# Second biases of the experts as a product per tile, four sets of buffers for the late sums, two Relu's on ScalarE, and a new order of the instructions

## What is computed

```python
# first layer, the recurrence, per token t and feature
tau = max(u + k, eps); e1 = exp(eps - tau); e2 = exp(u + k - tau)
out = (e1 * alpha + e2 * v) / (e1 * beta + e2)
tau2 = max(eps - w, k); d1 = exp(eps - w - tau2); d2 = exp(k - tau2)
alpha, beta, eps = d1 * alpha + d2 * v, d1 * beta + d2, tau2
# second layer, the experts
logits = flat_x @ W_router + b_router
top_vals, top_idx = top_k(logits, 2)
router_weights = softmax(sparse_logits)
for e in range(8):
    h = relu(flat_x @ W1[e] + b1[e])
    y = h @ W2[e] + b2[e]
    final_output += y * (router_weights[:, e] * mask)[:, None]
x = x + gb * final_output
```

## Time and profile before

| | |
|---|---|
| median of 3 runs | 1699.84 us (1699.17 to 1706.25) |
| the profiled execution | 1700.76 us, of which 1698.9 us from the first to the last instruction |
| mean granted TensorE clock | 0.889 |
| busy: PE, DVE, ACT, POOL | 1363.7, 1147.9, 968.7, 548.3 us |
| transfers | 217.67 MB |

### The profile page before, as it was taken

The page is one execution under the profiler, slowest core; times in us unless marked ns, Lnnn a source line. Parts: engine busy times, 40 slices in busy tenths (PEclk is TensorE's granted clock), DMA queues, the critical chain, the costliest instruction groups (busy, mean ns, idle before and its releaser), DMA issues. The chain is left out here.

```text
span 1698.9 us, 26885 instructions
## 1 busy us (share of the span) xinstructions
PE 1363.7 (80%) x8390; PEld 875.3 (52%) x8390; DVE 1147.9 (68%) x3024; ACT 968.7 (57%) x2279; POOL 548.3 (32%) x589
## 2 busy tenths in 40 slices
PE   3466887878879788999999878988999987983862
PEld 1233453434445335776666434556666655773761
DVE  4568788887989867758878887868674744141103
ACT  1344665656666456777777555656756654752440
POOL 1123221312132473122212236444151143325335
PEclk7677998979999878999999888799998998997995
DMA  4012134142211334555554222354645676887762
GB/s 120 7 35 72 37 121 157 47 129 68 89 52 47 89 103 124 155 164 161 146 177 133 71 76 75 108 155 132 176 136 152 174 202 191 268 267 239 213 198 63
DMA packets 202005, 217.67 MB, mean 128 GB/s; under 512 B 17402, under 2 KB 167493, under 8 KB 199560
## 3 DMA queue, kind: packets, MB, share of 16 engines
q1 hardware_dynamic: 193672, 199.17, 39.9%
q0 software_dynamic: 8192, 16.79, 3.1%
HBM read 161.18 MB, written 53.94 MB: 127 GB/s over the span
## 5 line engine op out<-in xcount | busy, mean ns | idle before, releaser
L1525 DVE TENSOR_REDUCE cmx<-bank 128x2 f32<-128x512 f32 x512 | 329.4, 683 | 94.4 <-PE bank L1148 80.2
L854 ACT ACTIVATE wide<-bank 128x512 f32<-128x512 f32 x512 | 278.9, 607 | 113.6 <-PE bank L1164 106.4
L1164 PE MATMUL bank<-wide 75*128 75x512 bf16 x512 | 182.5, 421 | 31.8 <-ACT wide L854 19.4
L1148 PE MATMUL bank<-wide 72*128 72x256 bf16 x1024 | 179.8, 285 | 29.3 <-DVE cmx L1525 23.0
L715 POOL DMA_INDIRECT x_slots<-sx,sslot x128 | 128.0, 1000 | 111.7 <-DMA x_slots<-sx,sslot 49.5
L1180 PE MATMUL bank<-wide,bva 128*32 128x512 f32 x1024 | 150.3, 668 | 14.6 <-ACT wide L854 9.6
L1148 PEld LDWEIGHTS bank<-wide 72*128 72x128 bf16 x1024 | 91.5, 101 | 131.6 <-issue 56.7
L734 POOL DMA_INDIRECT kg<-y_slots,sslot x104 | 101.2, 973 | 160.5 <-issue 49.6
L893 ACT ACTIVATE mH<-bank,mW 128x128 f32<-128x128 f32 x376 | 107.6, 375 | 55.6 <-PE bank L989 50.3
L1164 PEld LDWEIGHTS bank<-wide 75*128 75x128 bf16 x512 | 50.1, 106 | 154.8 <-ACT wide L854 84.6
L989 PE MATMUL bank<-mT,mW 128*128 128x128 f32 x872 | 122.8, 285 | 7.0 <-DMA mW<-in_wexp 2.2
(11 more groups left out here) (293 smaller groups left out, 2798.3 us busy)
## 6 DMA issues: line engine op xcount, KB each, us to landing
mW<-in_wexp SPq DMA_DIRECT2D x109, 514.0 KB
wide<-q_parts SPq DMA_DIRECT2D x32, 576.0 KB
inner<-in_wexp SPq DMA_DIRECT2D x31, 514.0 KB
wide<-in_wexp SPq DMA_DIRECT2D x16, 514.0 KB, 4.1
mX<-x_slots SPq DMA_DIRECT2D x27, 256.0 KB, 4.2
y_slots<-mX SPq DMA_DIRECT2D x27, 256.0 KB, 4.3
q_parts<-bp SPq DMA_DIRECT2D x32, 192.0 KB, 2.2
x_slots<-mH SPq DMA_DIRECT2D x2, 3072.0 KB, 10.9
```

What stands on the lines that cost most here:

```text
L854: act.activation(cP[:, i % 8, :], bank[seat["G_s", i]][:, :], ACT.Exp, scale=SCALE).then_inc(S["c_p"], 1)
L1148: ins = pe.matmul(ps[:, j * T:(j + 1) * T], cQ[0:SROWS, z, h, tt * P:(tt + 1) * P], cK[0:SROWS, z, h // G, :], start=True, stop=True)
L1164: pe.matmul(ps[:, :], cK[0:KROWS, z, g, sc_ * P:(sc_ + 1) * P], cQ[0:KROWS, z, h0:h0 + 2, :], start=True, stop=True).then_inc(S["c_s2"], 1)
L1525: dve.tensor_reduce(cmx[:, u % 2, tt, 2 * hp:2 * hp + 2], bank[seat["C_s", i]][:, :].rearrange("p (j t) -> p j t", j=2), AX_X, ALU.max, ne ...
```

## The change

1. The second biases. K_w, K_b and the copy between them are gone, 16 of each, and with them the first addition of K_out and the three operations of R_info that made weights by expert (L1600, L1602, L1604). In their place each tile gets one product of 24 rows in bf16, ahead of its M_d: the stationary operand is a column of a new array `which` (1 where the tile's expert is the row's), spread over 128 columns, the moving one is b2 as three bf16 parts. A step I_erow makes the parts at the start, and one more instruction in S_tile makes `which`.
2. The sets of the K stage. Chunks 0 to 9 use set 0; chunks 10, 11, 12, 13, 14 and 15 use sets 1, 2, 3, 0, 1 and 2. A gather waits only for the store of the last chunk in its own set, and the first use of sets 1 to 3 for the end of stage R_c of the last chunk.
3. E_y ends after the two differences. ACT makes Relu(z) and Relu(-z) and then both Exp's.
4. ORDER is another table on all engines.

```diff
-    "M": ("R_h R_lg S_pre K_w K_b M_t M_u".split(), (7,)),
+    "M": ("R_h R_lg S_pre M_t M_u".split(), (7,)),
...
+TURNS = FIRST_CHUNK[-2] - 1
+        k_sets = [max(c - TURNS, 0) % 4 for c in range(CHUNKS)]
         def k_set(c):
-            return (0, c + 1) if c <= LATE else (c - LATE, 1)
+            return k_sets[c], k_sets[:c + 1].count(k_sets[c])
...
                     if s == "K_g":
-                            if z == 0 and c:
-                                pool.wait_ge(S["k_st"], 16 * c)
+                            if n > 1:
+                                pool.wait_ge(S[f"k_st{z}"], 16 * (n - 1))
+                            elif z:
+                                pool.wait_ge(S["r_h0"], CHUNKS)
...
                     if s == "E_exp":
+                        act.wait_ge(S["e_ky"], i + 1)
+                        act.activation(aP[:, :, :, :], aQ[:, 1:3, :, :], ACT.Relu).then_inc(S["e_m"], 1)
                         act.wait_ge(S["e_m"], 2 * i + 1)
+                        act.activation(aQ[:, 1:3, :, :], aQ[:, 1:3, :, :], ACT.Relu, scale=-1.0).then_inc(S["e_m"], 1)
                         act.activation(aP[:, :, :, :], aP[:, :, :, :], ACT.Exp, scale=-1.0).then_inc(S["e_exp"], 1)
                         act.wait_ge(S["e_m"], 2 * i + 2)
-                        act.activation(aQ[:, 1:3, :, :], aQ[:, 1:3, :, :], ACT.Exp).then_inc(S["e_exp"], 1)
+                        act.activation(aQ[:, 1:3, :, :], aQ[:, 1:3, :, :], ACT.Exp, scale=-1.0).then_inc(S["e_exp"], 1)
...
                 def mlp_out(i, z, ps):
                     pe.wait_ge(S["m_r"], FC * (i + 1))
+                    g = place(i)[0]
+                    if i == FIRST_TILE[g]:
+                        pe.wait_ge(S["s_tile"], 2 * (g + 1))
+                    j = i - FIRST_TILE[g]
+                    pe.matmul(ps[:, 0:P], which[:, g, j:j + 1].broadcast_to([BROWS, P]), eb2[:, :],
+                              start=True, stop=False)
                     for c in range(FC):
-                                        weights[w_slot(i)[0]][:, o:o + D], start=(c == 0), stop=(c == FC - 1))
+                                        weights[w_slot(i)[0]][:, o:o + D], start=False, stop=(c == FC - 1))
...
                         dve.scalar_tensor_tensor(aQ[:, 2, :, :], aE[:, :, 0:T], negw[:, 0:1],
                                                  k_ps, ALU.add, ALU.subtract).then_inc(S["e_ky"], 1)
-                        dve.wait_ge(S["e_ky"], i + 1)
-                        dve.tensor_scalar(aP[:, :, :, :], aQ[:, 1:3, :, :], 0.0, None,
-                                          ALU.max).then_inc(S["e_m"], 1)
-                        dve.tensor_scalar(aQ[:, 1:3, :, :], aQ[:, 1:3, :, :], 0.0, None,
-                                          ALU.min).then_inc(S["e_m"], 1)
...
                     if s == "K_out":
-                        dve.wait_ge(S["k_b"], i + 1)
...
-                        v(dve.tensor_tensor(g_[:, 0, :, :], g_[:, 0, :, :], tiles(bank[seat["K_b", i]]), ALU.add))
...
 ORDER = {
...
-        K_b K_w K_b
+        W_d W_u W_d W_u W_d W_u W_d W_u W_d W_u W_d*2
```

More of the change, by code:

```diff
@@ L425, in program @@
             mask3 = rz[0:PARTS, 0, 0:PARTS]
+            eraw, eb_1, eb_2 = (rz[0:BROWS, k, :] for k in range(1, 4))
+            epart = cP[0:BROWS, 6, :].bitcast(BF16).rearrange("p (k d) -> p k d", d=D)[:, 0:PARTS, :]
+            esum = [cP[0:BROWS, 7, k * D:(k + 1) * D] for k in range(2)]
+            part_of = rhn[0:BROWS, 0, 0:PARTS]
+            turns = rhn[0:BROWS, 1, 0:BROWS]
             MOD = (3, 4, 5, 6)
@@ L454, in program @@
                 *[(colk[b * KR:(b + 1) * KR, :], rows_of_keys(a["cols"])) for b in range(BC)],
[L455 removed]
+                (rev[:, :], a["c_rev"]), (upper[:, :], a["c_upper"]),
+                *[(rz[k * EXPERTS:(k + 1) * EXPERTS, 1, :], a["L1_ffn_b2"]) for k in range(PARTS)],
                 (restart[:, :], a["c_restart"]), (steps16[:, :], a["c_steps16"]), (steps1[:, :], a["c_steps1"]),
@@ L622, in _ @@
                         sp.wait_ge(S["k_out"], i + 1)
-                        sp.dma_start(rows(a["out"], i), kg[k][:, 0, :, :]).then_inc(S["k_st"], 16)
-                sp.wait_ge(S["k_st"], 16 * CHUNKS)
+                        sp.dma_start(rows(a["out"], i), kg[k][:, 0, :, :]).then_inc(S[f"k_st{k}"], 16)
+                for k in range(4):
+                    sp.wait_ge(S[f"k_st{k}"], 16 * k_sets.count(k))
             @block.gpsimd
@@ L1235, in _ @@
                         mlp_out(LATE_TILE + i, 1 + (LATE_TILE + i) % 3, bank[seat["W_u", i]])
-                    if s == "K_w":
-                        pe.wait_ge(S["r_info"], i + 1)
-                        for t in range(NT):
-                            ins = pe.transpose(ps[0:EXPERTS, t * P:(t + 1) * P], rinfo[:, i, t, WT:WT + EXPERTS],
-                                               ident[:, :])
-                        ins.then_inc(S["k_tp"], 1)
-                    if s == "K_b":
-                        pe.wait_ge(S["k_wT"], i + 1)
-                        for t in range(NT):
-                            ins = pe.matmul(ps[:, t * P:(t + 1) * P], kwT[:, t * P:(t + 1) * P], eb2[:, :],
-                                            start=True, stop=True)
-                        ins.then_inc(S["k_b"], 1)
             @block.vector
@@ L1899 @@
-        K_sum K_out K_sum K_out K_sum K_out K_sum K_out K_sum K_out K_sum K_out K_sum K_out K_sum K_out
+        I_silu I_rows A_ln0s I_rows A_c A_ln1s I_col A_ln0s E_mix I_w I_brow E_scan E_y I_erow A_c E_wkv E_wkv1
+        E_wkv2 E_rec E_att E_x1 E_ln2s A_ln1s E_mix2 E_mix E_out E_scan E_y B_ln0s A_ln0s E_wkv E_wkv1 E_wkv2
+        E_rec A_c E_att E_x1 E_ln2s A_ln1s B_x2 B_ln1s E_mix2 B_q E_mix B_q B_k E_out B_v E_scan E_y B_ln0s
+        A_ln0s E_wkv E_wkv1 E_wkv2 E_rec E_att E_x1 E_ln2s C_s A_c C_s*2 A_ln1s B_x2 C_s B_ln1s C_s*8 E_mix2
@@ new lines @@
+        R_ln C_s B_q C_s*2 K_sum K_out B_k C_s*2 R_c C_s E_mix C_s*2 C_mp B_v C_s*5 E_out E_scan E_y B_ln0s
+        K_sum K_out E_wkv E_wkv1 C_s E_wkv2 E_rec C_s G_o E_att R_lg R_m1 C_s R_m2 E_x1 C_s E_ln2s C_s*2 R_e
+        K_sum C_s*2 K_out C_s E_mix2 C_s*2 R_info C_mp B_x2 C_s*4 B_ln1s C_s*6 G_o C_s*2 B_q C_s K_sum C_s*2
+        K_out C_s C_mp E_out B_q B_k G_o B_v B_ln0s G_o G_y K_sum C_s R_ln C_s K_out C_s*5 R_c C_s*5 G_o R_lg
+        R_m1 C_s*2 R_m2 C_s*2 C_mp B_x2 B_ln1s R_e G_o B_q*2 R_info B_k C_s*7 G_o C_s*9 C_mp G_o G_y R_ln C_s*8
@@ L1900 @@
+        R_c C_s*7 R_lg C_s R_m1 C_mp R_m2 R_e R_info S_cnt G_o S_base S_slot G_o S_tile C_s*5 G_o C_s*10 G_o C_s
+        C_mp C_s*2 B_v C_s G_y C_s*2 R_ln C_s*6 R_c C_s*5 C_mp G_o*2 R_lg G_o R_m1 R_m2 R_e G_o K_sum R_info
+        K_out G_y R_ln R_c R_lg R_m1 R_m2 R_e R_info S_cnt K_sum K_out S_base S_slot S_tile K_sum K_out K_sum
+        K_out K_sum K_out K_sum K_out K_sum K_out K_sum K_out K_sum K_out K_sum K_out K_sum K_out
         """,
```

464 lines of the change are left out of this document (237 added, 227 removed).

## The result

The changed kernel takes 1652.5 us (median of 4 runs, 1650.6 to 1659.8), the kernel before 1701.1 beside it. The ratio is 0.9718, with a 95% interval of 0.968 to 0.9755: 2.8% faster, 48 us. The forecast was 1669 with a range of 1640 to 1694. The profiled execution took 1651.28 us for a span of 1649.5.

The account below looks back on a forecast made before the run. No engine bounds the whole; DVE or PE leads by stretch, POOL's gather chain sets the end. Logits 1514.9 - 22 - 10 = 1482.9, scatters to 1532.3, gathers to 1659.9, end 1668.0: predicted 1669 us, range 1640 to 1694.

Parts of the forecast that it names:

- DVE's relief: Ahead of chunk 15's logits: less DVE work gains 15 us, a third let go for ACT's later first Exp, leaving 10.
- rival 3: ACT becomes the bound of the first 1430 us, its Relu's holding back the attention's Exp's and PE: 1725 us, chance 0.07.
- The order: Late tiles on PE ahead of the last logits fall from 26 to 15: 11 at 2.0 us, logits 22 us earlier.
- Biases: On PE ahead of the last logits: K_b and K_w save 15 us, the tiles' products cost 12; too little for a term.
- First to last scatter: POOL's scatters and gathers alternate by halves, each covering the other's landing: 34 us instead of 39.8, ending at 1532.3.
- The first scatter 1.4 us later behind the logits: Chunk 14's first scatter, 14.0 us behind the logits before, plus 1.4 for K_sum and K_out of chunk 6: 1498.3.
- One cycle of 24.3: POOL's gathers after the last scatter: 24.3 us to 1556.6, chunks 9 to 12 at 17.4, then 13.7 and 20, to 1659.9.
- a rival's cause: Rival 2, the end: late sets overlap nothing as transfers crowd and SP, in one row, is late: 1697 us, chance 0.13.
- What I said would show it: Changed profile: logits at about 1483, E_exp 4.2 us, no PE wait for K_out, no PE hole over 5 us from 1440.
- The relief rival: Rival 1: DVE's relief counts in full, ACT's Relu's lie beside other work, 33 us instead of 10: 1646 us, chance 0.20.

Follow-up runs that it names:

- The square: Kernel before with biases as product and four sets: old order -0.16% (max, min on DVE), +0.74% (Relu's on ACT); new order -2.06%, -2.82%.
- The run in the old order: Kernel before with only the biases as a product in each tile, K_w and K_b out, I_erow in: 1699.5 us, +0.03%.
- the last version of the end: Changed kernel with stores of chunks 7 and 8 earlier on SP, chunk 7's gather halves ahead of the last group's scatters on POOL: 1661.2 us, -2.29%.

## Why the forecast held, and where it did not

The time came within 1% of the forecast and on its side, but this is in part luck, since two errors of the sum went in opposite directions. The logits of chunk 15 came at 1442.3 us where I had 1482.9, 41 earlier, and from there to the end it took 207 us where I had 185, 22 more. In the one half the order was priced too low, in the other a wait was missing.

- **DVE's relief, -10 us: near in size, on the wrong grounds.** The step let a third of the relief go for ACT handing over the first Exp later, whatever the order. In the old order the later Exp gives DVE 16 of its 22.6 us back as waits, and PE waits 19 to 22 us more for ACT: the edit is worth +15 us there. That is rival 3's mechanism, the ACT row holding back PE. In the new order DVE waits 0.5 us for the Exp's, PE 4.5 us more for ACT, and the edit is worth -13. The step treated the order as if it only moved late tiles.
- **The order, -22 us: the term that failed.** I counted 11 late tiles behind the logits and nothing of the order ahead of that place. The square shows 60 us for it. The run with the new order up to 1328 us shows where: all of it before the last group, and the 11 tiles, whose move I priced, are in the part that is worth nothing. The slots of the third group came 33 us earlier, at 1326.1 against 1359.2, where my sum had 10. PE's idle time fell by 43 us; which of the moved steps brought it is not taken apart.
- **Biases, -3 us (-15 to +9): right.** The run in the old order gives 0 (-3 to +4). The single price was low: at the full clock the next product follows after 0.15 us (from 1443.26 to 1443.41 us in the trace of the changed kernel), not 0.11, and leaving it out gave 14 us in the new order. If it costs the same in the old order, K_w, K_b and the addition gave back about as much there. The Trainium skill (TensorE: Matmul & The Clock Gate, Back-to-back issue gap) gives 81 ns for a product of 128 columns in a stream with weight loads. This case's rows show nearly twice that from start to start, while the 14 us for 156 of them are 90 ns each.
- **First to last scatter 34 us: right,** 32.7.
- **The first scatter 1.4 us later behind the logits: right.** 15.6 us from the logits to the first scatter, where I had 15.4.
- **One cycle of 24.3, four of 17.4, then 13.7 and 20 us: right.** Measured 25.1, then 72.7 for four, 13.1 and 20.2, and 8.0 from POOL's last gather to the end.
- **The 19.8 us ahead of chunk 8's gather: missing in the sum.** The step said of scatter and gather that "one covers the other's landing" and went from the last scatter straight to the gather of chunk 8. I named SP "in one row" as a rival's cause, but did not follow K_st of chunk 7 along that row.
- **What I said would show it.** E_exp at 4.2 us, no wait for K_out on PE, and POOL waiting for stores only ahead of chunks 8 and 9 in the end: as said. No hole over 5 us on PE: wrong, there is one of 11.5.
- **The relief rival (0.20)** came nearer to the time for the wrong reason: 1646 by the whole relief of DVE, while the Relu's alone lose time.

For Relu's the Trainium skill (ScalarE: Activation LUTs, Rules for kernel authors) says VectorE and not ScalarE. Both orders bear on it. The old one agrees by 15 us. The new one, laid out for the longer way through ACT, goes 13 us against it, with an operation that still takes 1.06 us instead of 0.7.

That ACT waits for a product whose records had ended 12 us before remains open, and so does what it costs. It may have a part in the missing 19.8 us: in the same stretch SP waited 12.8 us, with no releaser seen either, before it could issue the next weights at 1491.7 us, and the store of chunk 7 stands behind these. No run took it out with all else kept.

## What to carry to other kernels

A move of work between engines in a kernel with a hand-written order can't be priced apart from the order: run the edit in the old order and the old edit in the new order before crediting either. Look first at how far the reader of the moved result stands behind it, on its own engine, and at what stands behind the moved work on its new engine. In both orders ACT had the same work and was busy for under 65% of the time; what told them apart were the waits of DVE and PE for it. At the end of a program, where POOL's chain, the tiles and SP's row are within some 10 us of each other, taking one wait away only shows the next one; the gain has to be looked for where the engines are really full.

## What the chip showed that was not expected

**A product that arrives late.** In the changed kernel ACT's copy of a late tile waits for a product whose matmuls, by their records, had ended (timeline of PE, then of ACT):

```profile
1473.93 0.28 PE L1022 MATMUL bank<-eb,which 24*128 24x128 bf16 x1 [3.89 <-issue]
1474.14 2.07 PE L1026 MATMUL bank<-mW,axr 128*128 128x128 f32 x8
```

```profile
1472.73 1.14 ACT L923 ACTIVATE axr<-bank,mW 128x128 f32<-128x128 f32 x4
1488.20 0.28 ACT L930 ACTIVATE mX<-bank 128x128 f32<-128x128 f32 x1 [14.33 <-remote]
```

Such a wait came in the same place in four other kernels that end in the new order (14.3, 14.4, 15.7 and 14.3 us), once with a second one of 14.1 us 55 us later, not in the last version of the end, and in none that ends in the old order. The stretches around it (windows):

```profile
1465.00:1472.00 7.00, 4.53 (x36) 3.90 (x34) 0.00 (x0) 1.31 (x5) 5.28 (x6) 1.00 0.92 281
1472.00:1493.00 21.00, 7.44 (x30) 6.29 (x30) 3.55 (x10) 3.15 (x12) 13.38 (x14) 0.51 0.29 94
```

The DMA share fell from 0.92 to 0.29 with the stall, and the granted clock from full speed to 0.51, which is 1.2 GHz. The records of matmuls are modelled and some are missing here, so what PE waited for can't be told from them.

**The same order takes a different time from one profile to another.** In the changed kernel and in four with the same order up to there the slots of the third group came at 1326.1, 1318.0, 1329.3, 1325.1 and 1325.0 us, a spread of 11 us, more than a moved word on SP was worth. Whether the kernel or the execution makes it is not shown: the four executions of the changed kernel alone lie 9 us apart. A difference of less than that between two profiles is to be looked for only behind the first place where they are meant to differ.
